# A GNN chain on one core: the bias b1a goes into the first table on TensorE, ScalarE empties the banks, and the accumulators are cleared ahead of the vote

## The reference, cut to what matters

```python
row, col = edge_index[0], edge_index[1]          # 106250 edges, sorted by col
h = jnp.concatenate([x[row], edge_attr], axis=1) # 128 + 128 columns
h = relu(h @ W1a + b1a) @ W1b + b1b              # W1a: 256 x 256, b1a: 256
summed = segment_sum(h, col, num_segments=x.shape[0])
```

## Time and profile before

| what | value |
|---|---|
| median of 3 runs | 4042.86 us (4042.48 to 4043.51) |
| the profiled execution's own time | 4043.53 us |
| its span, first to last instruction | 4041.3 us |
| granted TensorE clock, mean over the span | 0.944 of 2.4 GHz |
| busy: TensorE, VectorE, ScalarE, GpSimd | 89%, 52%, 42%, 70% |
| pass 0's first gather starts | 67.45 us |
| pass 0's last gather starts | 1126.4 us |

### The profile page before, as it was taken

The page is one execution under the profiler, slowest core; times in us unless marked ns, Lnnn a source line. Parts: engine busy times, 40 slices in busy tenths (PEclk is TensorE's granted clock), DMA queues, the critical chain, the costliest instruction groups (busy, mean ns, idle before and its releaser), DMA issues. The chain is left out here.

```text
span 4041.3 us, 72204 instructions
## 1 busy us (share of the span) xinstructions
PE 3616.4 (89%) x25086; PEld 2985.2 (74%) x25086; DVE 2094.7 (52%) x7560; ACT 1694.8 (42%) x4525; POOL 2828.7 (70%) x2958
## 2 busy tenths in 40 slices
PE   5999999999988999699996989999897789888987
PEld 4888888888865777466664777777675778787887
DVE  6888888888874222543334445555453133232232
ACT  1444444444442111311115555555564544445443
POOL 4777777777715777277774777777776777777776
PEclk8999999999998999799997999999998899999988
DMA  6666666666655676477772444444453445444443
GB/s 204 215 209 210 214 215 206 217 210 214 212 146 165 197 204 197 114 221 221 224 209 92 166 162 167 168 170 168 161 177 133 135 159 173 154 163 158 163 158 123
DMA packets 437486, 724.90 MB, mean 179 GB/s; under 512 B 68913, under 2 KB 289841, under 8 KB 436849
## 3 DMA queue, kind: packets, MB, share of 16 engines
q1 hardware_dynamic: 305984, 444.46, 33.2%
q0 software_dynamic: 107792, 249.49, 21.4%
q10 hardware_dynamic: 23330, 26.16, 1.9%
HBM read 527.20 MB, written 192.67 MB: 178 GB/s over the span
## 5 line engine op out<-in xcount | busy, mean ns | idle before, releaser
L604 POOL DMA_INDIRECT work<-table_rel,reli x1470 | 1389.3, 945 | 507.6 <-issue 444.3
L604 POOL DMA_INDIRECT work<-table_pre,srci x831 | 807.0, 971 | 269.6 <-issue 267.7
L1383 PE MATMUL bank<-work 128*128 128x72 f32 x2944 | 404.8, 297 | 181.1 <-DMA work<-table_rel,reli 181.1
L1383 PEld LDWEIGHTS bank<-work 128*128 128x128 f32 x2944 | 393.2, 212 | 219.5 <-DMA work<-table_rel,reli 213.9
L2256 ACT ACTIVATE work<-iota,local 128x72 f32<-128x72 f32 x1472 | 380.0, 342 | 364.5 <-PE bank L1383 353.5
L2261 ACT ACTIVATE work<-work,ew,src_lo 128x72 f32<-128x72 f32 x1472 | 517.6, 434 | 6.1
L1156 PE MATMUL bank<-work,acc 128*128 128x360 f16 x2574 | 440.1, 317 | 30.2 <-DVE acc L1505 18.0
L852 PE MATMUL bank<-w_both,work 128*128 128x256 f32 x1664 | 443.3, 392 | 18.0 <-DVE work L817 9.1
L604 POOL DMA_INDIRECT work<-table_mean,srci x311 | 302.7, 973 | 170.5 <-issue 87.8
L951 ACT ACTIVATE work<-work 128x512 f32<-128x512 f32 x416 | 252.2, 629 | 367.0 <-DVE work L817 363.9
L864 PEld LDWEIGHTS bank<-work 128*128 128x128 f32 x3328 | 398.6, 194 | 5.1 <-ACT work L951 0.2
(11 more groups left out here) (328 smaller groups left out, 5794.3 us busy)
## 6 DMA issues: line engine op xcount, KB each, us to landing
work<-adj SPq DMA_DIRECT2D x104, 720.0 KB
adj<-X SPq DMA_DIRECT2D x130, 450.0 KB
work<-ea_cols SPq DMA_DIRECT2D x208, 256.0 KB
kept<-work SPq DMA_DIRECT2D x50, 880.0 KB
kept<-w_both SPq DMA_DIRECT2D x50, 880.0 KB
work<-kept SPq DMA_DIRECT2D x50, 880.0 KB
w_both<-kept SPq DMA_DIRECT2D x50, 880.0 KB
work<-adj SPq DMA_DIRECT2D x52, 810.0 KB
```

What stands on the lines that cost most here:

```text
L604: pool.indirect_dma_start(into[:, u, :], None, tables[p], bass.IndirectOffsetOnAxis(ap=idx_of(p)[:, t:t + 1].bitcast(U32), axis=0)).then_i ...
L1383: mm = pe.matmul(bank[4 + m % LATE_BANKS][:, 0:PAIR_WIN], late_gat[n % LATE][:, u, :], late_hot[:, n % LATE_HOTS, u * PAIR_WIN:(u + 1) * P ...
```

## The change

- **b1a on TensorE.** VectorE splits b1a into three bf16 pieces whose sum is b1a to f32 precision: `b1a_parts` holds the first piece on partitions 0 to 31 and 96 to 127, the second on 32 to 63, the third on 64 to 95. `b1a_pick` (128x128 bf16) is one on partitions 0, 32 and 64 and zero elsewhere. The bf16 product of the two is b1a in every row, and it starts the sum in the bank; the f32 product of x and W1a is added to it.
- **ScalarE** copies the banks to `pre_rows` (three `ACT.Copy` for each chunk), and issues the store as before. VectorE's L451 is gone.
- **VectorE**: a new `start_dve_bias` (4 memsets, then 6 operations after b1a has landed) stands ahead of the votes; `start_dve_rounds` and `start_dve_edges` follow the votes directly.
- **GpSimd** clears `acc`, `hist` and `ones` before it waits for the votes.
- **The load of `w_all`** moves from the start of ScalarE's pass 0 to behind the relu of group 2.

```diff
@@ start_act_params, start_pe
             act.dma_start(bias[:, :], biases).then_inc(s_param, 16)
             act.dma_start(b2b_row[:, :], b2b.partition_broadcast(P)).then_inc(s_param, 16)
+
+        def start_act_weights(act):
             act.dma_start(w_all[:, :], weights).then_inc(s_param, 16)
...
             pe.wait_ge(s_weight, 32)
+            pe.wait_ge(s_prep, B1A_DONE)
...
-                pe.wait_ge(y_added, k * 3 + 3)
+                pe.wait_ge(y_copied, k * 3 + 3)
                 for t in range(CT):
-                    mm = pe.matmul(bank[3 * s + t // 2][:, t % 2 * HID:(t % 2 + 1) * HID], xT0[:, slot, t * P:(t + 1) * P],
-                                   w1a[:, 0, :], start=True, stop=True)
+                    into = bank[3 * s + t // 2][:, t % 2 * HID:(t % 2 + 1) * HID]
+                    pe.matmul(into, b1a_pick, b1a_parts, start=True, stop=False)
+                    mm = pe.matmul(into, xT0[:, slot, t * P:(t + 1) * P], w1a[:, 0, :], start=False, stop=True)
                 mm.then_inc(y_done, 1)
             quads(pe, body)
-
-        def start_dve_rows(dve):
+            pe.wait_ge(y_copied, CHUNKS * 3 + 6)
+
+        B1A_DONE = 10
+
+        def start_dve_bias(dve):
+            done(dve, dve.memset(b1a_pick, 0.0))
+            for i in range(3):
+                done(dve, dve.memset(b1a_pick[32 * i:32 * i + 1, :], 1.0))
             dve.wait_ge(s_weight, 32)
-
+            done(dve, dve.tensor_copy(b1a_parts, b1a_row[:, :]))
+            done(dve, dve.tensor_tensor(b1a_rest, b1a_row[:, :], b1a_parts, ALU.subtract))
+            done(dve, dve.tensor_copy(b1a_mid, b1a_rest))
+            done(dve, dve.tensor_tensor(b1a_rest, b1a_rest, b1a_mid, ALU.subtract))
+            done(dve, dve.tensor_copy(b1a_parts[32:64, :], b1a_mid[32:64, :]))
+            done(dve, dve.tensor_copy(b1a_parts[64:96, :], b1a_rest[64:96, :]))
+
+        def start_act_store(act):
             def body(k, slot, use):
                 s = slot % 2
-                dve.wait_ge(y_done, k + 5)
-                dve.wait_ge(table_stored[0][slot], use * 16)
+                act.wait_ge(y_done, k + 5)
+                act.wait_ge(table_stored[0][slot], use * 16)
                 for b in range(3):
                     n = 2 if b < 2 else 1
-                    dve.tensor_tensor(pre_rows[:, slot, 2 * b:2 * b + n, :],
-                                      bank[3 * s + b][:, 0:n * HID].rearrange("p (t h) -> p t h", t=n),
-                                      b1a_row[:, :].unsqueeze(1).broadcast_to([P, n, HID]), ALU.add).then_inc(y_added, 1)
-            quads(dve, body, lambda: start_dve_rounds(dve))
-
-        def start_act_store(act):
-            def body(k, slot, use):
-                act.wait_ge(y_added, k * 3 + 9)
+                    act.activation(pre_rows[:, slot, 2 * b:2 * b + n, :],
+                                   bank[3 * s + b][:, 0:n * HID].rearrange("p (t h) -> p t h", t=n), ACT.Copy).then_inc(y_copied, 1)
+                act.wait_ge(y_copied, k * 3 + 9)
                 act.dma_start(node_rows(tables[0], k), pre_rows[:, slot, :, :]).then_inc(table_stored[0][slot], 16)
             quads(act, body, lambda: start_act_sources(act))
@@ start_pool
+            pool.memset(acc[:, :, :], 0.0).then_inc(s_acc, 1)
+            pool.memset(hist[:, :], 0.0).then_inc(s_acc, 1)
+            pool.memset(ones[:, :], 1.0).then_inc(s_acc, 1)
+
             pool.wait_ge(s_vote, 3)
...
-            pool.memset(acc[:, :, :], 0.0).then_inc(s_acc, 1)
-            pool.memset(hist[:, :], 0.0).then_inc(s_acc, 1)
-            pool.memset(ones[:, :], 1.0).then_inc(s_acc, 1)
@@ start_dve_votes
+            start_dve_bias(dve)
             dve.wait_ge(s_const, CONSTANTS)
@@ pass0_act
                     relu(it * BODY, q, pre_added, relu_done)
+                    if it * BODY + q == 2:
+                        start_act_weights(act)
@@ vector
             start_dve_votes(dve)
-            start_dve_rows(dve)
+            start_dve_rounds(dve)
             start_dve_edges(dve)
```

More of the change, by code:

```diff
@@ L312, in gnn @@
         ratio = view(8960, 2, CH)
+        b1a_parts = more[:, 0:HID // 2].bitcast(BF16)
+        b1a_mid = more[:, HID // 2:HID].bitcast(BF16)
+        b1a_pick = more[:, HID:HID + P // 2].bitcast(BF16)
+        b1a_rest = bn_row[:, :, :].rearrange("p t c -> p (t c)")[:, 0:HID]
         staging_d = view(10240, TILES).bitcast(I32)
@@ L395, in gnn @@
         xT0_ready = sems("xT0_ready", 4)
-        y_done, y_added = sem("y_done"), sem("y_added")
+        y_done, y_copied = sem("y_done"), sem("y_copied")
         def start_sp(sp):
@@ L500, in start_dve_votes @@
         def start_dve_votes(dve):
-            dve.sem_inc(y_added, 6)
+            dve.sem_inc(y_copied, 6)
             for stored in table_stored[0]:
                 dve.sem_inc(stored, 16)
+            start_dve_bias(dve)
             dve.wait_ge(s_const, CONSTANTS)
```

## The result

The changed kernel takes 4032.93 us (median of 14 runs, 4031.34 to 4037.43), the kernel before 4042.07 (14 runs, 4037.59 to 4044.11). The ratio is 0.9979, interval 0.9971 to 0.9987: 9.1 us or 0.2% faster. The forecast was 4024.8 with a range of 4021.5 to 4032.5. The sign held; the gain is half of what I forecast, and the time lies just outside the range.

What follows compares the result with a forecast made beforehand. GpSimd's gather issue was taken to bound the kernel; the first gather moves from 67.45 to 49.35 us, 18.1 earlier. 4043.53 - 18.1 = 4025.4, less 0.7 to the median, gives 4024.8 us; range 4021.5 to 4032.5.

Steps and rivals of the forecast that it cites:

- GpSimd's issue sets pass 0: Pass 0: gathers start every 1.276 us at GpSimd's own pace, so an earlier first gather shifts the end equally.
- TensorE's chunk: Table stage: two f32 instructions and one bf16 product, five times a chunk, take 2.69 us; ten chunks 26.9 us.
- Its slow start: TensorE's clock begins at the lower level in its single burst, charged 2.5 us once.
- The bias operations: Six short VectorE operations ahead of the votes, some 2.2 us in all, taken as hidden.
- ScalarE's copies: Copies from the banks take 1.6 us a chunk, under TensorE's 2.69; two loads might delay TensorE, charged 0.8 us.
- The last store landed: Last store of the table, issued at 42.3 us, was forecast to land in 5.7 us, with ends 3.4 and 9.9.
- GpSimd clears from 14.2 for 16.35 + 0.5 us to 31.1, in a stretch where it only waited: Before the reductions: clearing fits GpSimd's waiting time, so votes end at 33.07 and reductions at 34.3 us, as before.
- the first rival: Clearing of acc stops VectorE: votes slip 16.3 us, first gather at 53.95, time 4029.4 us; chance 0.33.
- the 1.35 us from the last release to the first gather: Start of pass 0: the first gather follows the last store's landing, or `srci` in the rival, by 1.35 us.
- ScalarE was not the pace: Rival in the table stage: copies above 2.69 us a chunk; at 3.2 us the stage is 5 us longer, 4030; chance 0.10.
- TensorE's loads ran ahead: Rival on TensorE: exposed weight loads add 24 us over 50 products, kernel slower by 6 at 4048.7 us; chance 0.03.
- No effect: Rival: the shift is given back behind pass 0, time 4043 us; chance 0.04.

Runs made afterwards that it cites:

- e8_third_on_act: Changed kernel with two thirds of acc cleared on GpSimd after VectorE's operation 18, the last third on ScalarE; 0.9978 of the kernel before.
- e1_clear_late: Changed kernel with GpSimd's three clearings moved back behind its reductions; 0.9992 of the kernel before.
- e2_clear_first_only: Kernel before the change with only its three clearings moved ahead of GpSimd's wait for the votes; 1.005 of the kernel before.
- e5_two_windows: Changed kernel with GpSimd clearing two thirds of acc after VectorE's operation 18 and the rest after operation 41; 0.9969 of the kernel before.
- e3_pieces32: Changed kernel with acc cleared on GpSimd in 32 pieces instead of one memset; 0.9957 of the kernel before.
- e10_no_branch: Changed kernel without GpSimd's branch around the slow rounds of pass 0, which these inputs never enter; 0.9955 of the kernel before.
- e6_weights_early: Changed kernel with the load of w_all back at the start of ScalarE's pass 0; 0.9974 of the kernel before.
- e11_third_on_act_again: Repeat of the kernel with two thirds of acc cleared on GpSimd and the last third on ScalarE; 5275.93 us, 0.9983 of the kernel before.

## Why the prediction was wrong

**The steps that held.** GpSimd's issue sets pass 0 there, and the shift passes through: 8.3 us at the first gather, 9.3 at the last, 9.1 in the medians. TensorE's chunk measured 2.72 us against 2.69; the bf16 product adds 0.112 a pair against 0.107, so no weight load was exposed. Its slow start cost less than the 2.5 us charged: the first four pairs took 3.8 us instead of 2.2. The bias operations were hidden: the last ends at 9.4, ahead of TensorE's first product at 10.0. ScalarE's copies took 1.36 us a chunk against 1.6, and it held TensorE once, for 0.27 us, where I had charged 0.8. The last store landed in 3.7 us against 5.7. Taken by themselves, these would have put the first gather at 44.3 + 1.35 = 45.7; `e8_third_on_act`, where the stores come last, has 46.1. One reading of the page was off: GpSimd's 31% of the chain is six times the next engine's 5%, not three; nothing rests on it.

**The step that failed first** reads "GpSimd clears from 14.2 for 16.35 + 0.5 us to 31.1, in a stretch where it only waited". I asked only whether GpSimd had the time, and the sum charged nothing for what its clearing does to VectorE: it held the first cast for 16.68 us, and with it the votes, the rounds and `srci`, whose 12 us ahead of the table became 7.7 us behind it. I had this as the first rival, with 0.33, and it is what happened: `srci` done at 52.0, the rival said 52.6. `e1_clear_late` and `e2_clear_first_only` each move the clearing alone and the hold moves with it; `e5_two_windows` and `e8_third_on_act` keep the clearing early and it is gone.

I weighed two rows against each other, the 0.30 us of L505 and the 0.14 us of L573 in the midst of the memset. L505 deserved more weight than L573. Before, the cast ends 0.08 us after the `affine_select` beside it; in `e1_clear_late`, where it starts later against the same `affine_select` and takes 0.23 us, 0.09 after; in the changed kernel 0.08 after the last clearing. So the 0.30 fits a short hold, though it doesn't prove one. The one-column operations were not held in any of these traces (0.14 to 0.16 us beside a memset), so L573 said nothing of a cast of 128 columns. The rule of the Trainium skill that I cited (SBUF — State Buffer, section "Who interferes with whom") decided rightly: the cast and the wide `tensor_scalar` were held, the reduces and the adds were not. It speaks of one instruction; in `e3_pieces32` 32 of them in a row held VectorE as one.

**The term that was mis-sized**, in the forecast and in the rival alike, is the 1.35 us from the last release to the first gather. I took it from a kernel in which GpSimd had the load of the rounds and the branch behind it before the last store landed: `srci` was done at 56.5, the store whole at 66.1. Once the rounds come last, that way is exposed: 7.1 us, of which `e10_no_branch` puts 5.3 on the branch. The rival's own 52.6 + 7.1 gives 59.7 against the measured 59.1; with 1.35 it gave 53.95, 5.2 us too early, and close to the 54.2 of `e10_no_branch`, where the way is short. The 7.1 is read from the same trace, so the agreement is no second proof. That term carried the time out of the range: 4029.4 + 5.2 = 4034.6, less the 1 us more that was gained by the end of pass 0, is 4033.6, close to the 4032.93 measured.

**The other rivals.** ScalarE was not the pace, and TensorE's loads ran ahead. No effect did not occur. The weights' load in its new place costs nothing visible; in its old place, by the one profile of `e6_weights_early`, it would have cost some 2.7 us at the first gather, a gain of the change that the sum did not have.

## What to carry to other kernels

Work that is moved into an engine's idle time has to be checked against what the other engines run in that time, not only against the time itself: here a GpSimd clearing in an idle stretch held one VectorE cast for 16.7 us, and two waits on VectorE's progress were enough to place it without slowing VectorE, at the price that GpSimd itself came late to its next work. A latency read from a trace in which an engine was early says nothing of that engine's own way; when another release becomes the last one, add the way from there, with loads of registers and branches, before the next visible instruction. And a wait taken off the path shows the next one at once: behind 16 us of votes stood 7 us of GpSimd, and only then the stores.

## What the runs showed that I had not expected

- 32 GpSimd memsets of 0.59 us without a wait between them held a VectorE cast for 17.93 us; it did not get in between any two.
- GpSimd's first reduction over partitions started 5.9, 6.2 and 6.7 us after its last memset (`e5_two_windows`, `e8_third_on_act`, `e11_third_on_act_again`), though VectorE's votes were done by then, with no releaser shown. The cause stays open.
- Three chips ran the same kernel before in 5247 to 5311 us instead of 4042, with a granted TensorE clock of 0.84 to 0.85 over the span instead of 0.944, and with the first 60 us nearly the same.
